# Memory stage of a hybrid block: the out-projection moved between the state products and the next step's first products

## The reference, cut to what matters

```python
for c0 in range(0, S, CHUNK):              # CHUNK = 128, eight chunks
    g = grad(W_state, k[:, sl], v[:, sl]) * GRAD_SCALE       # per token
    g = g * jnp.minimum(MAX_GRAD_NORM / gn, 1.0)
    (S_state, W_state), Wtraj = jax.lax.scan(step, (S_state, W_state), xs)
    h = jax.nn.silu(jnp.einsum('btd,btod->bto', q[:, sl], W1t))
    outs.append(jnp.einsum('bto,btpo->btp', h, W2t))
retrieved = jnp.concatenate(outs, axis=1)
out = retrieved @ Wo.T                      # the out-projection
out = out * jax.lax.rsqrt(jnp.mean(out * out, -1, keepdims=True) + EPS) * norm_g
return out * gate
```

## Time and profile before

| | |
|---|---|
| median of 3 runs (lowest to highest) | 1180.2 us (1175.94 to 1180.26) |
| the profiled execution's own time | 1180.01 us |
| its span, first to last instruction | 1177.9 us |
| mean granted TensorE clock | 0.955 of full speed |
| TensorE matmul busy over the span | 1080.8 us (92%) |
| VectorE, ScalarE, GpSimd busy | 1006.4, 803.7, 229.2 us |
| o4: L1539, 64 matmuls, all in the memory stage | 1021.8 to 1149.8 us |

### The profile page before, as it was taken

One profiled execution on the slowest core, in us unless ns is written; L12 is line 12 of the kernel. 1 busy time (PEld: TensorE's weight loads), 2 busy tenths in 40 slices (PEclk: granted clock), 3 DMA queues, 4 the chain that ended last, 5 costly groups with the idle time before them and its releaser, 6 DMA issues. The chain is left out here.

```text
span 1177.9 us, 22167 instructions
## 1 busy us (share of the span) xinstructions
PE 1080.8 (92%) x8566; PEld 598.0 (51%) x8566; DVE 1006.4 (85%) x1591; ACT 803.7 (68%) x1628; POOL 229.2 (19%) x295
## 2 busy tenths in 40 slices
PE   5997799999999999999999999966999987999974
PEld 4884233333333333333333333335777756889864
DVE  6877999999999999999999999614699998488875
ACT  4452388888888888888888888941766765434431
POOL 6514200000000000000000000032333223556541
PEclk9997699999999999999999999987999997999997
DMA  7693404422441344044224400121234236433401
GB/s 266 158 341 148 55 13 74 66 49 38 74 66 31 55 66 63 23 73 66 46 41 74 72 21 13 42 94 59 83 102 146 77 117 205 116 113 100 131 19 53
DMA packets 87317, 101.56 MB, mean 86 GB/s; under 512 B 21868, under 2 KB 57196, under 8 KB 87212
## 3 DMA queue, kind: packets, MB, share of 16 engines
q1 hardware_dynamic: 86380, 98.56, 34.8%
q10 hardware_dynamic: 832, 1.58, 0.4%
HBM read 55.09 MB, written 43.88 MB: 84 GB/s over the span
## 5 line engine op out<-in xcount | busy, mean ns | idle before, releaser
L653 ACT ACTIVATE prob<-ps_s 128x512 f32<-128x512 f32 x1024 | 555.9, 597 | 115.1 <-PE ps_s L723 97.6
L674 DVE TENSOR_REDUCE maxes<-ps_m 128x2 f32<-128x1024 f32 x512 | 606.7, 1219 | 17.9 <-PE ps_m L712 14.7
L735 PE MATMUL ps_o<-prob,v_ones 128*32 128x256 f32 x4096 | 327.9, 392 | 8.0 <-issue 6.9
L723 PE MATMUL ps_s<-q_stack,k_stack 64*128 64x512 f32 x1024 | 261.4, 500 | 0.0
L712 PE MATMUL ps_m<-k_stack,q_stack 62*128 62x512 f32 x1024 | 219.0, 421 | 14.8 <-DVE maxes L674 11.0
L723 PEld LDWEIGHTS ps_s<-q_stack,k_stack 64*128 64x128 f32 x1024 | 99.7, 184 | 211.1 <-ACT prob L653 186.6
L735 PEld LDWEIGHTS ps_o<-prob,v_ones 128*32 128x32 f32 x4096 | 81.8, 108 | 191.8 <-issue 100.8
L712 PEld LDWEIGHTS ps_m<-k_stack,q_stack 62*128 62x128 f32 x1024 | 101.1, 192 | 31.6 <-DVE maxes L674 24.1
L615 POOL COPY v_ones<-v_all 128x512 f32<-128x512 f32 x16 | 9.8, 613 | 531.2 <-PE ps_o L735 531.2
L1120 DVE TENSOR_TENSOR x_all<-x_all,p_a 128x512 f32<-128x512 f32 x16 | 11.0, 686 | 49.1 <-PE p_a L1204 49.1
L69 DVE BATCH_NORM_STATS2 p_stats<-x_all 128x6 f32<-128x256 f32 x128 | 44.9, 413 | 7.1 <-DMA x_all<-in_x_dram 6.2
(11 more groups left out here) (247 smaller groups left out, 1477.0 us busy)
## 6 DMA issues: line engine op xcount, KB each, us to landing
qk_parts<-p_parts SPq DMA_DIRECT2D x32, 512.0 KB, 7.3
q_stack<-qk_parts SPq DMA_DIRECT2D x96, 128.0 KB, 4.7
k_stack<-qk_parts SPq DMA_DIRECT2D x96, 128.0 KB, 7.8
oT<-o_sb SPq DMA_DIRECT2D x32, 256.0 KB, 4.0
x_all<-in_x_dram SPq DMA_DIRECT2D x8, 512.0 KB, 10.0
heads<-oT SPq DMA_DIRECT2D x16, 256.0 KB
inverse<-inverse_sums SPq DMA_DIRECT2D x16, 256.0 KB
out_dram<-x_all SPq DMA_DIRECT2D x8, 512.0 KB, 3.2
```

The source lines that it names most:

```text
L653: act.activation(prob[at % P_RING][:, h], ps_s[:, (GH * at + h) % S_RING], ACT.Exp, scale=HD ** -0.5).then_inc(exp_done, 1)
L674: dve.tensor_reduce(maxes[:, i // 2, i % 2], ps_m[:, i % M_PAIRS], AX.X, ALU.max).then_inc(m_taken, 1)
L723: pe.matmul(ps_s[:, (GH * (UNITS * slot + KT * qc + kt) + h) % S_RING], r32(k_st[slot][rows, pair, kt * P:(kt + 1) * P]), r32(q_st[slot][r ...
L735: ins = pe.matmul(ps_o[32 * h:32 * h + 32, queries], v_st[slot][:, kt, h], prob[(UNITS * slot + KT * qc + kt) % P_RING][:, h, queries], st ...
```

## The change

In TensorE's list of the memory stage, o4(c-1) is issued behind c4(c) and ahead of c1(c+1), instead of behind c1(c+1). Where c4 and c1 are not issued (step 7) nothing moves, and step 0 has no o4. So it is in effect in steps 1 to 6, six times. No instruction is added or removed, and no wait is changed.

```diff
@@ def on_tensor(pe), the loop over the steps @@
             if valid(c + 1):
                 c4(c)
-                c1(c + 1)
             if valid(c - 1) and valid(c):
                 o4(c - 1)
+            if valid(c + 1):
+                c1(c + 1)
```

## The result

| | before | after |
|---|---|---|
| median (lowest to highest), 14 runs each | 1180.23 us (1175.92 to 1183.06) | 1185.01 us (1182.65 to 1187.08) |
| ratio after to before, 95% interval | | 1.0045 (1.0031 to 1.0059) |
| span of the profiled execution | 1177.9 us | 1184.0 us |
| end of c4(1) to end of c4(6), TensorE's timeline | 96.31 us | 99.88 us |

The kernel is slower by 4.8 us in the medians. The interval of the ratio lies wholly above 1 and makes the loss 3.7 to 7.0 us. It is less than the 0.5% (5.9 us) that I had named as the least that can be told, so by my own measure this is "same", to which I had given 0.39, and not "slower", to which I had given 0.58. The forecast was 1186.5, and its 6.5 us lie inside the interval.

A forecast was written before the change was run, and what follows sets the result against it. TensorE's list bounds the memory stage, with one stop per step where ffn waits for VectorE's zT_lo. Losses of 1.35 (step 2), 1.11 (step 3), 3.24 (steps 4 to 6) and 0.83 (step 7) make 6.5: 1180.0 becomes 1186.5 us, range 1182 to 1191.

The forecast's parts named there:

- the chains: Work behind late c1: ScalarE's squares and sigmoid delay o2 by 0.83 us; GpSimd's scale_h delays dz and ffn by 1.08.
- The case that I held likeliest: Full sum of the step losses over the memory stage, time 1185.9 to 1188 us, chance 0.50.
- the sum: Losses of steps 2 to 7 added: 1.35 + 1.11 + 3.24 + 0.83 = 6.5 us.
- GpSimd's chain: Slope to scale_h, 1.08 us late in step 4, holding VectorE's L1774 and so dz, zT_lo and ffn.
- I take nothing: Clock term set to zero; half-speed stretches in steps 3 to 7 would cost 1.6 us each, 8.0 in all.
- The smaller loss: Rival: only o2's late release counts, 6 x 0.83 = 5.0 us, time 1185.0; chance 0.23.
- The clock as a loss: Rival: new half-speed stretches in steps 3 to 7, 1189.7 us with two, 1194.5 with five; chance 0.13.
- No loss: Rival: h ready by 8.0, second sigmoid late by less than 1.1 us, so 1180.0 or 1177.8; chance 0.11.

The follow-up runs named there:

- e1: Changed kernel with ScalarE's mean squares of o4 put behind the second sigmoid; profiled once, steps 3 to 6 took 20.2 us.
- e2: Changed kernel with GpSimd's inverse root of the mean square put behind its inverse norms; profiled once, steps 3 to 6 took 19.93 us.
- e3: Changed kernel with both reorderings, ScalarE's mean squares and GpSimd's inverse root put later; 1179.99 us, ratio 0.9999 to the kernel before.
- e6: Kernel before with an added, unused GpSimd tensor_tensor reading SBUF behind scale_h in steps 2 to 6; steps 4 to 6 took 19.56 us.
- e5: Kernel before with ScalarE's mean squares behind the second sigmoid and GpSimd's inverse root behind the inverse norms; 1179.27 us, ratio 1.0014.
- e7: Kernel before with two unused GpSimd memsets that read nothing behind scale_h; profiled once, steps stayed at 19.2 us.

## Why the prediction was right, and where it was off

The direction, the chains and the size of a steady step came out, and the time lies in the stated range. The case that I held likeliest (1185.9 to 1188) was missed by 0.9 us. The times alone can't tell 4.8 from 6.5 us; the profiles can, and they show terms that the sum had wrong, above all in step 2.

**The chains.** Nearly every offset came out: c1 1.83 late, the sigmoid that aT needs at 3.98 (3.99), slope at 4.44 (4.45), scale_h ending at 11.57 (11.56), dz at 11.51 (11.51), zT_lo at 13.23 (13.22), ffn at 14.65 (14.64) in step 4; c4(2) 1.32 late (1.35). e1, e2 and e3 show that both chains are real and each is enough to cost a step most of its loss: with ScalarE's put right alone the step is still 0.99 us too long, with GpSimd's alone 0.72, with both 0.04.

**Smaller than said.** o2 was 0.67 late, not 0.83, and idle for 0.42, not about 0.8, since the second sigmoid comes 0.13 earlier than 7.52 and TensorE answers `h` faster than I took; GpSimd's chain being longer, nothing came of that. A step lost 0.99 and not 1.08 to 1.11: ffn is 1.09 late, but o4 follows c4 0.09 us closer than c1 did. In four steps that is 3.96 instead of 4.35.

**Right size, wrong route.** Step 7 lost 0.82 at ffn, as forecast (0.83), but not through turn and copy_zT, which came 0.73 later: through the squares of the errors on ScalarE, L1775 and dz, as e2 shows for the steps before.

**The term that was off** is the clock in step 2. I let c4(2) keep its half-speed stretch ("I take nothing") and looked only for new ones. There were none in steps 3 to 7 up to their last ffn, and the one in c4(2) went: c4(2) took 3.65 us instead of 5.37. So step 2 counts 1.32 - 1.72 = -0.40 where the sum had +1.35. The sum as measured: -0.40 + 3.96 = 3.56 from the end of c4(1) to the end of c4(6), against 99.88 - 96.31 = 3.57 in the profiles; and behind it 62.6 us before and 63.6 after to the end of the span, as the means of three profiles each, so +1.0, where 0.8 is step 7's and the rest lies in half-speed stretches of the drain (the steps behind the last c4) that differ from profile to profile. Step 1 gives back 0.1, since o4 follows c4(1) closer than c1 did. 3.6 + 1.0 - 0.1 = 4.5, and the medians differ by 4.8.

**The rivals.** The smaller loss named the measured time (1185.0), and that is luck: its reason was that GpSimd does not hold L1774, and GpSimd does. The clock as a loss did not come in steps 3 to 7; in step 2 it came as a gain. No loss is refuted as the kernel stands, and e3 shows that its condition, a second sigmoid early enough, is one of two that it would take.

**Open:** why c4(2) is at full speed behind the changed list. The wait before it is 1.83 us there and 2.11 in the kernel before, but e3 was at half speed behind 1.89 us, e2 behind 2.51 (c4(2) starting at 15.20) and e6 behind 2.60, while e1 was at full speed behind 1.18 and e5 behind 2.12 (c4(2) at 14.09). In the nine profiles that share step 2 with one of the two kernels the clock went with the arrangement. That the arrangement decides it is not shown: e5 went against it, and c4(1) changed between executions of the same kernel. The rule was not found, and a forecast should carry these 1.7 us as a term that may fall either way.

## What to carry to other kernels

Work that is independent still pays for its place: ahead of o1, o4 gave the other engines 1.83 us for what c1 starts; ahead of c1 it gave them nothing. Before moving such a piece, follow every consumer of what is made late to the end of each in-order list, and look for instructions queued ahead of the critical one that could stand behind it (here the mean squares and an inverse root); turned first, they made the move free here. And look for short instructions of one engine that end together with a long one of another, and for longer ones that last longer than elsewhere beside it: that is a dependency which no wait shows.

## What the hardware showed that I had not expected

A VectorE instruction on four columns lasted up to 1.14 us instead of 0.16 beside a reading GpSimd tensor_tensor (e1), while one with a PSUM input took its usual 0.69 us inside such an instruction (L1833), and memsets held nothing (e7). The profile shows a held instruction as busy, and it ends behind GpSimd's by 0.02 us on four columns, 0.08 on 64 and 1.07 on 1024. The half-speed stretch of one stage was there in five of five profiles and gone in four of four with c4(2) 1.3 us later, worth 1.72 us, more than the loss that the move caused in that step. In c4(1) the same kernel had it in two profiles and not in the third, worth 1.62 us.
